# Sampling and deformable products of an image embedding in one stage

## The reference, cut to what matters

```python
h = leaky_relu(batchnorm(conv2d(x, stem_w, stem_b, 4)))        # 96 channels, 24x24
offset = conv2d(h, off_w, off_b, 4)                            # 16 taps x 2, 6x6
...
sampled = v00*(1-wy)*(1-wx) + v01*(1-wy)*wx + v10*wy*(1-wx) + v11*wy*wx   # bilinear, per tap
out = einsum('bckhw,ock->bohw', sampled, w.reshape(O, C, 16)) + b         # 192 channels
h = leaky_relu(batchnorm(out))                                 # -> 36 tokens of 192 per image
...
q = clip(round(w / scale), -127, 127) * scale                  # fake-quantised text rows
h = concatenate([h, quant_weight[x_txt]], axis=1)
```

## Time and profile before

| | us |
|---|---|
| median of three runs | 2387.16 |
| the profiled execution, own time | 2391.56 |
| its span, first to last instruction | 2389.8 |
| stem and offsets, to the first position load of sampling | 0 to 86.27 |
| sampling, to the first product over samples | 86.27 to 269.28 |
| deformable products, to the attention's first product | 269.28 to 324.01 |
| attention and splines | 324.01 to the end |

### The profile page before, as it was taken

How to read it: one execution, slowest core, us unless ns; L and a number is a source line. 1 busy time by engine, 2 the same in 40 slices (tenths; PEclk the granted TensorE clock), 3 DMA queues, 4 the chain that set the end, 5 groups by cost and what they waited for, 6 DMA issues and landing times.

```text
span 2389.8 us, 49107 instructions
## 1 busy us (share of the span) xinstructions
PE 2277.9 (95%) x20033; PEld 2134.9 (89%) x20033; DVE 1846.9 (77%) x2241; ACT 1411.4 (59%) x1391; POOL 302.1 (13%) x169
## 2 busy tenths in 40 slices
PE   6599989999999989999999999979999999999999
PEld 5366777888888789999999999979999999999999
DVE  7699756666666587776767766579999999999995
ACT  6488303444444554435435345399888888888881
POOL 7622000000000021322322321000000000000000
PEclk9799998999999889999999999989999999999999
DMA  6655241111111101111111110210000000000000
GB/s 206 179 155 149 67 153 28 51 47 48 48 47 48 36 26 47 42 46 53 46 50 45 49 52 24 88 62 24 23 23 23 23 23 23 23 23 23 23 19 10
DMA packets 115454, 129.98 MB, mean 54 GB/s; under 512 B 17063, under 2 KB 106167, under 8 KB 115127
## 3 DMA queue, kind: packets, MB, share of 16 engines
q1 hardware_dynamic: 95215, 103.54, 14.5%
q10 hardware_dynamic: 16520, 14.34, 2.0%
q0 software_dynamic: 3616, 10.54, 1.7%
HBM read 92.79 MB, written 35.58 MB: 54 GB/s over the span
## 4 chain that ended last, share of the span: by engine, by line
PE 62%; ACT 1%; DVE 0%; issue 0%; ACTq 0%
PE spline_acc L1981 20%; PE spline_acc L1950 10%; PE spline_acc L1949 10%; PE spline_acc L1951 9%; PE spline_acc L1977 9%; PE spline_acc L1978 4%; PE spline_xT L764 0%; ACT spline_s L1842 0%; ACT spline_weights_split L1869 0%; DVE spline_f L1715 0%; ACT spline_t L778 0%; ACT spline_t L780 0%; ACT spline_front L778 0%; ACT spline_front L780 0%; ACT spline_t L782 0%
## 5 line engine op out<-in xcount | busy, mean ns | idle before, releaser
L1950 PE MATMUL spline_acc<-spline_f,spline_weights_high 128*128 128x328 f32 x1536 | 483.3, 315 | 0.0
L1949 PE MATMUL spline_acc<-spline_f,spline_weights_high 128*128 128x328 f32 x1536 | 480.6, 313 | 2.5 <-DVE spline_weights_low L1698 2.5
L1951 PE MATMUL spline_acc<-spline_f,spline_weights_low 128*128 128x328 f32 x1536 | 477.1, 311 | 0.0
L1981 PE MATMUL spline_acc<-spline_weights,spline_f 128*128 128x192 f32 x2214 | 382.7, 327 | 0.0
L1981 PEld LDWEIGHTS spline_acc<-spline_weights,spline_f 128*128 128x128 f32 x2214 | 356.8, 190 | 0.0
L1949 PEld LDWEIGHTS spline_acc<-spline_f,spline_weights_high 128*128 128x128 f32 x1536 | 290.7, 189 | 2.8 <-DVE spline_weights_low L1698 2.8
L1950 PEld LDWEIGHTS spline_acc<-spline_f,spline_weights_high 128*128 128x128 f32 x1536 | 289.6, 189 | 0.0
L1951 PEld LDWEIGHTS spline_acc<-spline_f,spline_weights_low 128*128 128x128 f32 x1536 | 289.3, 188 | 0.0
L1977 PE MATMUL spline_acc<-spline_weights_split,spline_f_high 128*128 128x384 f32 x861 | 274.0, 382 | 14.8 <-DVE spline_f L1726 14.8
L1715 DVE SCALAR_TENSOR_TENSOR spline_f<-spline_front 128x984 fp32r<-128x984 f32 x128 | 148.0, 1196 | 93.6 <-PE spline_acc L1951 88.3
L1978 PE MATMUL spline_acc<-spline_weights_split,spline_f_low 128*128 128x192 f32 x861 | 217.8, 253 | 0.0
(11 more groups left out here) (240 smaller groups left out, 4894.4 us busy)
## 6 DMA issues: line engine op xcount, KB each, us to landing
spline_front<-pos_scr SPq DMA_DIRECT2D x32, 540.0 KB, 4.4
hid_scr<-spline_hid SPq DMA_DIRECT2D x64, 164.0 KB, 1.8
spline_xn<-hid_scr SPq DMA_DIRECT2D x41, 256.0 KB, 3.1
attend_spread<-rec_scr SPq DMA_DIRECT2D x128, 61.5 KB, 2.2
pix_scr<-spline_front SPq DMA_DIRECT2D x32, 225.0 KB, 3.3
spline_weights_raw<-w SPq DMA_DIRECT2D x1, 6144.0 KB, 21.4
spline_step_to<-w SPq DMA_DIRECT2D x36, 128.0 KB, 2.1
spline_step_from<-w SPq DMA_DIRECT2D x36, 128.0 KB, 2.1
```

What stands on the lines that cost most here:

```text
L1949: nc.tensor.matmul(z, high, x_high, start=start, stop=False)
L1950: nc.tensor.matmul(z, high, x_low, start=False, stop=False)
L1951: last = nc.tensor.matmul(z, low, x_high, start=False, stop=stop)
L1981: last = nc.tensor.matmul(z, rest[:, cols], w2[:, i, r - SETS, :], start=False, stop=stop)
```

## The change

- Sampling and deformable products become one block. TensorE, written out in full, forms tile t behind image BEHIND[t], which is two images behind the last image that the tile reads: tiles 0 to 8 stand behind images 5, 9, 12, 16, 19, 23, 26, 30 and 31.
- VectorE makes a tile's tokens behind the weights of image BEHIND[t] + 2, and a text chunk behind each of the first five (chunks 3 to 7). The tokens have a ring of four. SyncE's stores of tokens and text stand between its loads, six images behind BEHIND[t].
- Text chunk 1 moves into the offset stage, chunk 2 is formed where chunk 1 was.
- VectorE's clip of `hx` (L547) goes; ScalarE makes |x - column| first and, after the five |y - row|, relu(1 - |x - column|). The weights' sign turns, and `store` copies with scale -1.

```diff
@@ sample_phase @@
+    LAST = [((t + 1) * P - 1) // VIS for t in range(VT)]
+    BEHIND = [min(n + 2, B - 1) for n in LAST]
...
+        mix = ps("deform_acc", [P, 4, 512])
...
+            def leave(t):
+                sp.wait_ge(tok_ready, t + 1)
+                sp.dma_start(vis_scr[t * P:(t + 1) * P, :], tok[:, t % 4, :]).then_inc(tok_out[t % 4], 16)
+                if t < len(chunks):
+                    text.store(sp, chunks[t])
...
+            for b in range(2, B):
+                sp.wait_ge(dist, b - 1)
+                load(b)
+                for t in range(VT):
+                    if BEHIND[t] + 6 == b:
+                        leave(t)
...
-                s.mark(nc.vector.tensor_scalar(hx[u][0:PIXC, :], hx[u][0:PIXC, :], 1.0, 1.0, ALU.min, ALU.subtract))
                 s.run(nc.vector.tensor_scalar(dy[u][0:PIXC], dy[u][0:PIXC], 1.0, 1.0, ALU.min, ALU.subtract))
...
+            def token(t):
+                s = Step(dve, step, 3 * t)
+                dve.wait_ge(mixed, t + 1)
...
+                s.run(nc.vector.tensor_tensor(y, mix[:, t % 4, 0:D], rows[:, 0, :], ALU.mult))
+                s.run(nc.vector.tensor_tensor(y, y, rows[:, 1, :], ALU.add))
+                s.run(nc.vector.scalar_tensor_tensor(y, y, SLOPE, y, ALU.mult, ALU.max))
+                dve.sem_inc(tok_ready, 1)
+                if t < len(chunks):
+                    text.form(nc, dve, chunks[t])
+
+            text.form(nc, dve, chunk)
+            for b in range(B):
+                weigh(b)
+                for t in range(VT):
+                    if BEHIND[t] + 2 == b:
+                        token(t)
...
+                nc.scalar.activation(hx[u][0:PIXC, :].rearrange("p (k n) -> p k n", k=TAPS), p[:, 1],
+                                     ACT.Abs, bias=neg[0:PIXC, NPIXC:NPIXC + 1]).then_inc(apart, 1)
                 for part in range(NPIXC):
...
+                act.wait_ge(apart, 2 * t + u + 1)
+                nc.scalar.activation(hx[u][0:PIXC, :], hx[u][0:PIXC, :], ACT.Relu, bias=1.0, scale=-1.0
+                                     ).then_inc(dist, 1)
...
+            def deform(t):
+                pe.wait_ge(stored, LAST[t] + 1)
...
+                    last = nc.tensor.matmul(mix[:, t % 4, 0:D], samp_all[0:C1, kk, t * P:(t + 1) * P],
+                                            w[0:C1, kk, :], start=(kk == 0), stop=(kk == TAPS - 1))
...
+            for b in range(B):
+                image(b)
+                for t in range(VT):
+                    if BEHIND[t] == b:
+                        deform(t)
...
@@ tokens @@
-            offset_phase(nc, c, inv, shift, hT_all, pixel_out, room[:, RING * (n + PADPIX):], pos_scr, text, (0,))
+            offset_phase(nc, c, inv, shift, hT_all, pixel_out, room[:, RING * (n + PADPIX):], pos_scr, text, (0, 1))
...
-            sample_phase(nc, c, front, text.spare, pos_scr, pix_scr, samp_all, text, (1,))
-            deform_phase(nc, c, w_dcn, samp_all, vis_scr, text, range(2, text.CHUNKS))
+            sample_phase(nc, c, front, text.spare, pos_scr, pix_scr, samp_all, w_dcn, vis_scr, text, 2,
+                         range(3, text.CHUNKS))
```

More of the change, by code:

```diff
@@ L485, in _, with sample_phase @@
             dve.wait_ge(rows_ready, 1)
-def sample_phase(nc, c, front, spare, pos_scr, pix_scr, samp_all, text, chunks):
+def sample_phase(nc, c, front, spare, pos_scr, pix_scr, samp_all, w, vis_scr, text, chunk, chunks):
     S2 = SAMPLES // 2
+    LAST = [((t + 1) * P - 1) // VIS for t in range(VT)]
+    BEHIND = [min(n + 2, B - 1) for n in LAST]
     with ExitStack() as stack:
@@ L508, in sample_phase @@
         stored = sem("sample_stored")
+        mixed, step = sem("deform_product"), sem("deform_step")
+        tok_ready, tok_out = sem("deform_ready"), [sem(f"deform_out{u}") for u in range(4)]
         block = stack.enter_context(nc.Block())
@@ L512, in _, with load @@
         def _(sp):
-            def load(b, u):
-                sp.dma_start(pos[u][0:PIXC, :], pos_scr[bass.ds(b, 1), :].rearrange("a n -> (a n)")
-                             .partition_broadcast(PIXC)).then_inc(pos_in[u], 16)
-            for u in range(2):
-                load(u, u)
-            for n in chunks:
-                text.store(sp, n)
-            with sp.Fori(1, B // 2) as t:
-                for u in range(2):
-                    sp.wait_ge(dist, 2 * t + u - 1)
-                    load(2 * t + u, u)
+            def load(b):
+                sp.dma_start(pos[b % 2][0:PIXC, :], pos_scr[b:b + 1, :].rearrange("a n -> (a n)")
+                             .partition_broadcast(PIXC)).then_inc(pos_in[b % 2], 16)
+            def leave(t):
[3 more added lines that the diff above has]
+                    text.store(sp, chunks[t])
+            for b in range(2):
+                load(b)
+            text.store(sp, chunk)
+            for b in range(2, B):
+                sp.wait_ge(dist, b - 1)
+                load(b)
+                for t in range(VT):
+                    if BEHIND[t] + 6 == b:
+                        leave(t)
+            for t in range(VT):
+                if BEHIND[t] + 6 >= B:
+                    leave(t)
+            for t in range(VT - 4, VT):
+                sp.wait_ge(tok_out[t % 4], 16 * (t // 4 + 1))
+            for u in range(2):
+                sp.wait_ge(text.out[u], 16 * (text.CHUNKS // 2))
         @block.gpsimd
@@ L595, in _, with image @@
         def _(pe):
-            def image(t, u, first):
-                pe.wait_ge(h_in[u], 16 * t + 16)
-                pe.wait_ge(weights, 2 * t + u + 1)
-                if not first:
-                    pe.wait_ge(stored, 2 * t + u - 1)
+            def image(b):
+                u = b % 2
+                pe.wait_ge(h_in[u], 16 * (b // 2) + 16)
+                pe.wait_ge(weights, b + 1)
+                if b >= 2:
+                    pe.wait_ge(stored, b - 1)
                 for half in range(2):
```

80 lines of the change are left out of this document (20 added, 60 removed).

## The result

The changed kernel took 2403.96 us in the median of 20 executions, the kernel before, beside it, 2394.85 us in 20: a ratio of 1.0038, 95% interval 1.0020 to 1.0055, so some 9 us slower. The forecast was 2390.5 us with a range to 2402: the time lies just above the range, slower where no change was forecast. The profiled execution has a span of 2401.9 us.

What follows compares the result with a forecast made beforehand. VectorE was taken to bound sampling at 5.2 us per image and to end the deformable stage late. Delays of 0.9, 0.3, 2.8, 13.5 and 1.0 us put the last token at 325.2 against 321.9: +3.3, forecast 2390.5 us, range 2377 to 2402.

Steps and rivals of the forecast that it cites:

- The reading of the kernel before: Sampling is set by VectorE at 5.2 us per image; in the deformable stage VectorE ends 5.6 us after TensorE.
- the bound of 15 us on any gain: Merged stage: if TensorE never waited, 205.2 us of products instead of 221.7, so at most some 15 us gained.
- Offset stage, +0.9: Text chunk 1 in the offset stage makes positions leave 0.7 to 1.2 us later; taken as +0.9.
- First image, +0.3: Before image 0, ScalarE's seven passes, relu at 0.76 us, less VectorE's saved 0.37: net +0.3 us.
- ScalarE's pace: 5.3 us per image against TensorE's 4.86 idles TensorE at images 2 to 5, 26, 29 and 30: 2.8 us.
- The five waits: TensorE waits for VectorE behind each text chunk between images, 2.7 us five times: 13.5 us.
- Rival A: The text chunks between images are hidden after all, the 13.5 us do not appear: 2377 us, chance 0.2.
- Rival B: The five stalls also lower TensorE's clock, each up to 1.7 us more: 2392 to 2399 us, chance 0.22.
- The end: Image 31's product must be stored before tile 8 can start: 1.0 us.
- Attention was not to move by more than 3 us: Sign that the mechanism is wrong: the attention stage, which the change does not touch, moves by more than 3 us.
- The sum: Last token at 325.2 us against 321.9, +3.3; added to the 2387.2 us median it gives 2390.5 us.
- some 19 us come out of the merging: Merged stage: separate barrier, VectorE's text tail and 0.3 us per image saved; about as much goes back.

Runs made afterwards that it cites:

- experiment 5: Kernel before, chunk 1 formed in offset stage: its store moved to sampling's start (first, 2382.33 us), both stores moved (2392.55), or chunk formed behind the convolution (2387.14).
- experiment 2: The changed kernel without forming text chunks 3 to 7, their stores kept: 2398.30 us, ratio 1.0008.

## Why the prediction was wrong, point by point

**The reading of the kernel before** held: VectorE's round in sampling and its text tail set the stage's length, and the bound of 15 us on any gain stood. The shortest stage of a variant with spread halves is 213.9 us, where 205.2 was the least.

Two steps of the forecast failed: the offset stage's term, which priced VectorE alone, and the term for the stalls, which priced the idle time and left the clock out. Only the second shows in every profile of the changed kernel.

**Offset stage, +0.9: the first step that failed.** Its working was for VectorE alone, and that was right: where the convolution was short (clip on VectorE, first profile, with the convolution starting at 65.6 us as before), VectorE's own work ended at 82.61 and L480 stood at 82.53, against a forecast of 82.8 and 81.98 in the earlier trace rows. Its timeline:

```profile
82.20 0.41 DVE L477 SCALAR_TENSOR_TENSOR attend_wv_low<-attend_wv_low,attend_rest_low,attend_wv 128x192 fp32r<-128x192 f32 x1
82.53 0.51 DVE L480 SCALAR_TENSOR_TENSOR spline_front<-offset_acc,offset_bias,offset_grid 128x288 f32<-128x288 f32 x1
```

The step said that "what hid this chunk is an idle VectorE". It took TensorE's 16.3 us beside it as given; in 9 of 15 profiles they became 24 to 25, and then L480 waits for TensorE (7.64 us above). Bounds of 0.7 and 1.2 left no room for that. In the mean over those profiles it is 8.5 x 9 / 15 = 5 us; how often it is long in executions without a profile isn't known.

**First image, +0.3:** from the first load of positions to the first image 14.1 to 14.2 us in the changed kernel's three profiles, 13.9 and 14.3 before. The two profiles of the kernel before differ by as much as the term, so it is neither confirmed nor refuted. The relu's row is 0.68 us, for 0.76.

**ScalarE's pace:** image 5 stands 5.28 us behind image 4, and tile 0 4.93 us behind image 5; forecast 5.3. The term of 2.8 us came out at 2.6, but not as worked out: 0.94 at image 3, where TensorE waits 0.78 us for pixels, 0.36 and 0.42 behind it, 0.07 at the tile, and 0.78 in one piece at image 30, with nothing at 26 and 29. The sum was right partly by luck.

**The five waits:** 2.52, 2.58, 2.51, 2.57 and 2.52 us at images 8, 12, 15, 19 and 22, together 12.7 for 13.5. Place, number and size are as worked out. The rows show the mechanism; the changed kernel's timeline at image 12:

```profile
168.53 0.96 DVE L197 TENSOR_TENSOR spline_weights_raw<-spline_weights_raw 128x768 f32<-128x768 f32 x1
...
169.40 1.65 DVE L570 TENSOR_SCALAR spline_front<-spline_front 120x2880 f32<-120x2880 f32 x1
171.09 3.16 DVE L573 TENSOR_TENSOR hat_weights<-spline_front,spline_weights_raw 120x2880 f32<-120x2880 f32 x1
...
174.35 2.88 PE L647 MATMUL sample_acc<-hat_weights,spline_x 120*96 120x288 f32 x11 [2.58 <-issue]
```

The chunk ends, clip and multiply follow with nothing between them, and TensorE starts 0.10 us behind the multiply (174.25). Rival A is out. One of its grounds was miscounted: the 201 us of VectorE count six chunks, but one of these stands ahead of the first image, so that only five are inside, 195 us.

**Rival B came true, and this is the second step that failed**: the forecast's 13.5 us for the text chunks between images took the stalls as idle time alone and left their clock to a rival with a chance of 0.22. What the runs show: three of five waits had a fall of the clock behind them in each of the three profiles of the changed kernel, of 3.4 us each, at a price of 1.4 to 1.7 us, forecast at up to 1.7. Together 4.8 us, which with the forecast's 223.8 gives 228.6 us of stage for 228.2, 227.7 and 228.0 measured. The argument against it (TensorE is busy on both sides of the wait) was wrong: the clock fell three times with TensorE busy on both sides. The Trainium skill (TensorE: Matmul & The Clock Gate, HAM oscillation) speaks of such falls from gaps between bursts, and these traces agree: a gap of 2.5 us had one behind it in three cases of five.

**The end:** 0.74 us for 1.0 (the wait for the last image's samples). Right.

**Attention was not to move by more than 3 us.** It did: 543.4, 540.5 and 534.3 us, against 533.5 and 533.8. Nothing of it is touched, and the lengths go by TensorE's clock in its first 110 us. The windows from 330 to 440 us, of the changed kernel, of the kernel before repeated, and of that with spread halves and the store moved, repeated:

```profile
330.00:440.00 110.00, 102.50 (x1418) 89.44 (x1417) 56.86 (x135) 33.76 (x55) 4.07 (x4) 0.84 0.26 88
```

```profile
330.00:440.00 110.00, 101.80 (x1506) 88.05 (x1505) 62.54 (x145) 38.20 (x62) 4.06 (x4) 0.92 0.27 90
```

```profile
330.00:440.00 110.00, 101.97 (x1609) 88.97 (x1609) 66.82 (x159) 40.24 (x64) 4.19 (x5) 1.00 0.27 92
```

Over all 20 profiles attention takes 525.4 us plus 0.43 of the time spent at the low clock in those 110 us (6 to 37 us of it), with a correlation of 0.97. Whether the stage before it sets how long that is, stays open: the changed kernel and its variant with the store moved had 534 to 543 (five profiles, mean 539.7), the four with spread halves 526.7 to 535.4, but other kernels without a stall in the stage, as the first in experiment 5, had 541.0 too.

**The sum.** The forecast started from a median of 2387.16 us in three runs; in 20 executions the kernel before has 2394.85. So of the 13.5 us by which the changed kernel's median lies above the forecast, 7.7 are that start and only 5.8 are the difference, +9.1 us for +3.3. The words under the forecast's sum, that some 19 us come out of the merging, don't fit it: by its terms 15.2 come out (221.7 against 205.2 and 1.3 for the tokens), and 18.5 go back.

Of the 22.4 us between the two profiles that are like for like, 8.3 are the convolution, 6.3 the stage (4.2 more than forecast, about what rival B's falls of the clock cost), 6.7 attention. The three pairs of medians differ by 9 to 14 us, less than the two profiles do; neither the long convolution nor the long attention is in every profile. Also the kernel before has its share of chance: 118 executions of it beside these runs had mean clocks of 0.973 to 0.983, and those at 0.981 took 2382.3 us in the mean, those at 0.976 2398.1.

**Is there a version that beats both?** The four timings with spread halves (chunk 1 in the offset stage, store moved or not) have ratios of 0.9999, 0.9986, 0.9972 and 0.9983, in the mean 0.9985, about 3.6 us under the kernel before; one of the four intervals leaves out 1. Moving the chunk alone, without merging (0.9989), can't be told from it.

## What to carry to other kernels

A piece of work moved under an idle stretch of one engine may be paid for on another that runs there: price it also by what the busy one beside it may lose, here 8 us in 9 of 15 profiles. Where two engines of nearly equal load feed one another through a ring of two, work of 6 us in one lump between the rounds stalls the other each time, and cutting it into halves, placed away from the other extra work, took 11 to 14 us of the stage back with no work removed. And a forecast of a stall has to have the clock's price in it as a term, not as a rival, as soon as the trace shows one fall behind a gap of that size.

## What the runs showed of the hardware that was not expected

- A matmul sequence in four column groups (96 rows by 32 columns each) runs four abreast in 0.49 us, and for 9 to 10 us at a time fell to one after another at 0.7 us each, in 9 of 15 profiles in which VectorE had work throughout, and never in 5 in which it had less.
- The fifth gather in the stem was held for 32.8 us in 14 of 20 profiles and took no more than 2.5 in the other six, of the changed kernel among others, where the convolution starts 9 to 14 us earlier. What holds it is not shown. The timelines of GpSimd, in the kernel before and in the changed one:

```profile
20.30 32.83 POOL L201 DMA_INDIRECT spline_weights_raw<-table,text_index  x1 [1.15 <-PE by_pixel L357]
```

```profile
20.47 1.60 POOL L201 DMA_INDIRECT spline_weights_raw<-table,text_index  x1 [0.30 <-issue]
```

- Falls of the clock last 3.4 us or a multiple of it in these traces. Behind waits of 2.5 us there was one in three of five cases, images 15, 19 and 22 in four profiles and 8, 15 and 22 in a fifth; a wait of 1.77 us in experiment 2 had one behind it, and the wait of 1.91 or 1.92 us at image 30 in the four profiles with spread halves had one in two of them and none in the other two.
